# Feed-forward's beginning in a fused attention and FP4 feed-forward kernel: weight pieces turned in order of use, ten before the first gate unit and 24 among the first tile's gate matmuls

## The reference, cut to what matters

```python
x = x + attention(layernorm(x))            # 16 heads, causal, then @ W_O
x = x + ffn(layernorm(x))
def fp4_linear(x, w):                      # x (b, s, k), w (n, k)
    return einsum('bsk,nk->bsn', fp4_quant_dequant(x), fp4_quant_dequant(w))
gate = fp4_linear(x, w_gate)               # w_gate, w_up: 1408 x 512
y = fp4_linear(x, w_up)
h = silu(gate) * y
ffn = fp4_linear(h, w_down)                # w_down: 512 x 1408
```

## Time and profile before

| | us |
|---|---|
| median of 3 runs (lowest, highest) | 3051.26 (3050.97, 3052.30) |
| profiled execution: own time | 3052.97 |
| profiled execution: span in the trace | 3051.2 |
| PE busy in the span | 2989.1 (98%) |
| DVE busy | 2622.9 (86%) |
| ACT busy | 1350.4 (44%) |
| POOL busy | 755.0 (25%) |
| feed-forward's first PE instruction | 1275.29 after the start |

### The profile page before, as it was taken

One profiled execution on the slowest core, in us unless ns is written; L12 is line 12 of the kernel. 1 busy time (PEld: TensorE's weight loads), 2 busy tenths in 40 slices (PEclk: granted clock), 3 DMA queues, 4 the chain that ended last, 5 costly groups with the idle time before them and its releaser, 6 DMA issues.

```text
span 3051.2 us, 65181 instructions
## 1 busy us (share of the span) xinstructions
PE 2989.1 (98%) x23204; PEld 2208.6 (72%) x23204; DVE 2622.9 (86%) x4209; ACT 1350.4 (44%) x2010; POOL 755.0 (25%) x680
## 2 busy tenths in 40 slices
PE   7999899999999999889999999999999999999999
PEld 6787644444444444478888888888888888888887
DVE  7999788889889888888888888888888888888886
ACT  5666577877777787532222222222222222222221
POOL 3444200000000000023333333333333333333332
PEclk9999899999999999999999999999999999999999
DMA  7889856655655665521111111111111111101110
GB/s 244 283 289 300 275 123 143 149 133 137 154 133 138 149 137 137 151 84 32 38 42 42 42 35 35 42 41 42 42 33 36 42 42 41 42 30 40 42 35 15
DMA packets 247628, 304.20 MB, mean 100 GB/s; under 512 B 21968, under 2 KB 154960, under 8 KB 247504
## 3 DMA queue, kind: packets, MB, share of 16 engines
q1 hardware_dynamic: 247504, 302.88, 35.8%
HBM read 190.35 MB, written 112.46 MB: 99 GB/s over the span
## 4 chain that ended last, share of the span: by engine, by line
PE 56%; DVE 1%; ACT 0%; DMA 0%; issue 0%; POOL 0%; SPq 0%; DVEq 0%
PE p_ring L1845 20%; PE p_ring L1873 16%; PE ps_od L1845 11%; PE ps_od L1825 5%; PE p_ring L1863 3%; PE p_ring L1853 1%; DVE sb_wg_lo L1751 0%; PE ps_od L1873 0%; PE p_ring L1825 0%; PE p_ring L1888 0%; DVE sb_fp_tmp L102 0%; DVE sb_wd_lo L1751 0%; DMA dn<-sb_fp_tmp 0%; DVE sb_h_amax L88 0%; DVE sb_stage L1722 0%
## 5 line engine op out<-in xcount | busy, mean ns | idle before, releaser
L1040 ACT ACTIVATE sb_probs<-scores 128x1024 f32<-128x1024 f32 (+3 forms) x512 | 405.8, 840 | 113.7 <-PE scores L1246 107.3
L788 POOL TENSOR_TENSOR sb_at_in<-sb_at_in,sb_inv_in 128x512 f32<-128x512 f32 x64 | 89.0, 1390 | 1069.0 <-DMA sb_inv_in<-dinv 1068.3
L1845 PE MATMUL p_ring<-sb_wg_hi,sb_xq_hi 128*128 128x512 f32 (+1 forms) x1024 | 295.2, 369 | 0.3 <-DVE sb_wd_lo L1751 0.3
L1548 POOL TENSOR_TENSOR sb_stage<-sb_stage,sb_h_inv 128x512 f32<-128x512 f32 (+1 forms) x192 | 210.8, 1098 | 339.2 <-DVE sb_h_inv L94 339.2
L1845 PE MATMUL p_ring<-sb_wg_lo,sb_xq_hi 128*128 128x512 f32 (+1 forms) x1024 | 290.5, 365 | 0.0
L1845 PE MATMUL p_ring<-sb_wg_hi,sb_xq_lo 128*128 128x512 f32 (+1 forms) x1024 | 289.9, 364 | 0.0
L1873 PE MATMUL p_ring<-sb_wd_hi,sb_ht_hi 128*128 128x512 f32 x693 | 275.9, 398 | 0.0
L1246 PEld LDWEIGHTS scores<-sb_q_hi,sb_k_hi 32*128 32x128 f32 x1536 | 73.7, 182 | 278.3 <-ACT sb_probs L1040 154.6
L1873 PE MATMUL p_ring<-sb_wd_hi,sb_ht_lo 128*128 128x512 f32 x693 | 270.2, 390 | 0.0
L1873 PE MATMUL p_ring<-sb_wd_lo,sb_ht_hi 128*128 128x512 f32 x693 | 269.8, 389 | 0.0
L1554 POOL TENSOR_TENSOR sb_stage<-sb_stage,sb_h_scale 128x512 f32<-128x512 f32 (+1 forms) x192 | 190.0, 989 | 267.4 <-DVE sb_stage L104 267.4
(11 more groups left out here) (203 smaller groups left out, 7172.3 us busy)
## 6 DMA issues: line engine op xcount, KB each, us to landing
kq<-sb_kq_out SPq DMA_DIRECT2D x32, 1024.0 KB, 7.2
sb_kq_raw<-kq SPq DMA_DIRECT2D x64, 512.0 KB, 6.8
sb_xin<-in_L_attn_x_dram SPq DMA_DIRECT2D x32, 512.0 KB, 6.9
v<-sb_v_out SPq DMA_DIRECT2D x64, 256.0 KB, 6.5
rq<-sb_r_out SPq DMA_DIRECT2D x64, 256.0 KB, 4.4
sb_qr<-rq SPq DMA_DIRECT2D x32, 512.0 KB
sb_kr_hi<-kr SPq DMA_DIRECT2D x32, 512.0 KB
sb_kr_lo<-kr SPq DMA_DIRECT2D x32, 512.0 KB
```

Of the source, the lines that this page charges most:

```text
L1040: act.activation(probs(k)[:, 2 * pair:2 * pair + 2, off:BANK], scores[(2 * k + pair) % RING2][:, :, off:BANK], ACT.Exp, scale=SCALE).then_ ...
L1548: pool.tensor_tensor(x, x, spread(h_inv[:, a // QB:b // QB], (b - a) // QB), ALU.mult).then_inc(h_y, 1)
L1845: i = pe.matmul(ps[:, m, 0:b0 - a0], xt[a][:, c, :], wg[b][:, m, c, a0:b0], start=(c == 0 and a == b == 0), stop=(c == DC - 1 and a == 1))
```

## The change

The pieces are reordered, so that gate and up pieces for hidden columns 0 to 511 come first (pieces 0 to 7), then those for 512 to 1023 (8 to 15), then the rest (16 to 21); the down pieces stay last. Ten pieces (`ALONE`) are turned in the phase of their own, which now ends with `turn_x(0, 0)`. The other 24 are turned inside tile 0's gate units (`AMONG`): six in G0 (one every two passes), ten in G1 and eight in G2 (one before each of the first passes). Each gate unit waits for the pieces that it needs (`NEEDED`: 8, 16; G2 waits for 26). The wait for all 34 moves to G1 of tile 1. Pieces from 16 on use only the four late slots. G2's pieces use two other banks, and piece 27 waits for the bank of G0.

ACT and DVE get the pieces in matching places of their lists: on ACT, eight pieces stand between `magic_h(0, 0, 0)` and `round_attention(0, 2)`; on DVE, 26 and 27 stand behind `hidden(0, 0, 1)`, and 28 to 33 behind `round_hidden(0, 0, 0)`. For tile 0 POOL runs `hidden_y` of unit 0 before `divide`. SP stores the last rows of attention (which share tiles with `x_to_y`) behind the load of piece 9 instead of 11.

```diff
-FIRST_LATE = 28
-LATE = {28: 7, 29: 8, 30: 9, 31: 10, 32: 2, 33: 1}
+FIRST_LATE = 16
+ALONE = 10
+AMONG = [(ALONE, 16), (16, 26), (26, 34)]
+NEEDED = [8, 16, 22]
...
-    return LATE[n] if n >= FIRST_LATE else n % PREP_SLOTS
+    return PREP_SLOTS + n % LATE_SLOTS if n >= FIRST_LATE else n % PREP_SLOTS
...
-        self.jobs = [(m, r, 0, D) for m in range(2) for r in range(FC)]
+        self.jobs = [(m, r, 0, D) for rows in (range(4), range(4, 8), range(8, FC)) for m in range(2) for r in rows]
...
-            return ring[n % RING3 if n < GATE_JOBS else 1 + n % 2][:, 1]
+            return ring[n % RING3 if n < ALONE else 1 + n % 2 if n < AMONG[2][0] else 2 + n % 2][:, 1]
...
-                if n == 11:
+                if n == 9:
                     sp.wait_ge(o_copied, 1)
                     sp.dma_start(t["at"][B * GROUPS - 1, :, BANK:S], last_o[:]).then_inc(last_stored, 16)
...
+                if flags(q, r)[0]:
+                    hidden_y(q, r, 0)
                 if exists(q, r + 2):
                     divide(q, r + 2)
-                hidden_y(q, r, 0)
+                if not flags(q, r)[0]:
+                    hidden_y(q, r, 0)
...
-            for n in range(GATE_JOBS):
+            for n in range(ALONE):
                 round_job(n)
...
-                if n == 8:
+                if n == 6:
                     magic_x(0, 0)
-                if n == 15:
-                    round_x(0, 0, (0, -1))
+            round_x(0, 0, (0, -1))
...
                 if first:
-                    for n in range(GATE_JOBS, 25):
+                    for n in range(ALONE, 14):
                         round_job(n)
                 if exists(q, r + 1):
                     magic_x(q, r + 1)
                 if first:
-                    for n in range(25, FIRST_LATE):
+                    for n in range(14, AMONG[1][0]):
                         round_job(n)
                 silu_of(q, r, 0)
...
                 if first:
-                    for n in range(FIRST_LATE, len(jobs)):
+                    for n in range(*AMONG[1]):
                         round_job(n)
                 silu_of(q, r, 1)
                 magic_h(q, r, 0)
+                if first:
+                    for n in range(*AMONG[2]):
+                        round_job(n)
                 if exists(q, r + 2):
                     round_attention(q, r + 2)
                 silu_of(q, r, 2)
...
-                if n == 9:
+                if n == 7:
                     x_to_q(0, 0)
-                if n == 17:
-                    rest_of_x(0, 0, (0, -1))
+            rest_of_x(0, 0, (0, -1))
...
                 if first:
-                    for n in range(GATE_JOBS, 24):
+                    for n in range(ALONE, 13):
                         rest_of_job(n)
                 if following:
                     x_to_y(q, r + 1)
                 if first:
-                    for n in range(24, FIRST_LATE):
+                    for n in range(13, AMONG[1][0]):
                         rest_of_job(n)
                 hidden(q, r, 0)
                 if first:
-                    for n in range(FIRST_LATE, 30):
+                    for n in range(AMONG[1][0], 19):
                         rest_of_job(n)
                 if following:
                     x_to_q(q, r + 1)
...
                 if first:
-                    for n in range(30, len(jobs)):
+                    for n in range(19, AMONG[2][0]):
                         rest_of_job(n)
                 hidden(q, r, 1)
+                if first:
+                    for n in range(AMONG[2][0], 28):
+                        rest_of_job(n)
                 round_hidden(q, r, 0)
+                if first:
+                    for n in range(28, len(jobs)):
+                        rest_of_job(n)
                 hidden(q, r, 2)
...
-                if flags(q, r)[0] and s == 2:
+                if flags(q, r)[0]:
+
+                    pe.wait_ge(lo, AMONG[2][0] if s == 2 else NEEDED[s])
+                if isinstance(q, int) and (q, r, s) == (0, 1, 1):
...
-                        if flags(q, r)[0] and s < 2 and at % 2 == 0:
-                            turn_weights(GATE_JOBS + 6 * s + at // 2)
+                        if flags(q, r)[0] and s == 0 and at % 2 == 0:
+                            turn_weights(AMONG[0][0] + at // 2)
+                        if flags(q, r)[0] and s > 0 and at < AMONG[s][1] - AMONG[s][0]:
+                            turn_weights(AMONG[s][0] + at)
...
-                if n >= GATE_JOBS:
-                    pe.wait_ge(lo, max(GATE_JOBS, n - 1))
+                if n == AMONG[2][0] + 1:
+
+                    pe.wait_ge(ps_free, number(0, 0, "G0") + RING3 + 1)
+                elif n >= ALONE:
+                    pe.wait_ge(lo, max(ALONE, n - 1) if n != AMONG[2][0] else n)
...
-            for n in range(GATE_JOBS):
+            for n in range(ALONE):
                 turn_weights(n)
                 if n == 3:
                     project(0, 0, (0, -1))
-                if n == 13:
-                    turn_x(0, 0, (0, -1))
-            pe.wait_ge(lo, GATE_JOBS)
+            turn_x(0, 0, (0, -1))
```

## The result

| | before | after |
|---|---|---|
| median, six runs each on one chip (lowest, highest) | 3051.16 (3049.13, 3053.57) | 3061.97 (3057.34, 3064.26) |
| ratio, 95% interval | | 1.0033 (1.0021 to 1.0046) |
| profiled execution: own time | 3052.97 | 3057.34 |
| profiled execution: span | 3051.2 | 3055.5 |

The account below looks back on a forecast made before the run. DVE was taken to bound the stretch the change touches, PE everything from 1337.5 on. Leads of 6.7, 6.2 and 1.2 us became 5.8 and 9.0 late, then +6.8: span 3058.0, median 3058.1; sum's range 3055.5 to 3060.5, wider 3052.5 to 3062.

Parts of the forecast that it names:

- Signs of being wrong: `hidden` of unit 1 before 1322, a clock of 0.50 inside G1, or `divide` ending before G2 does.
- Phase alone: Stretch up to `residual(0, 1)`: it starts at 1299.0 instead of 1305.71, a lead of 6.7 us.
- G0: Tile 0's first gate unit: ends 1.5 us later; `hidden(0, 0, 0)` at 1310.35 instead of 1316.56, lead 6.2.
- G1: Second gate unit, ten pieces: waits of pieces spend 5 of 6.2 us; lead 1.2 at `hidden(0, 0, 1)`.
- G2: Third gate unit, now eight pieces: ends at 1336.3 against 1330.5, 5.8 us late.
- Tile 2's inputs: Loads queued behind piece 33's: `divide` starts at 1337.8, HT0 of tile 1 at 1346.55, 9.0 us late.
- Given back: HT0 and G0 of tile 1 at full clock take 6.55 instead of 8.81 us, leaving +6.8 us.
- The store: In the phase alone: stored behind piece 9's load, it frees `x_to_y` sooner, 1.0 us saved.
- from there on all as before: Behind HT0 of tile 1, nothing changes up to the kernel's end.
- rival (a): Clock also falls in gaps inside G1 and G2: 2.4 us more, 3060.5; chance 0.24 including late loads.
- rival (c): Faster: the 18 pieces behind G0 hide under matmuls, the 6.2 us lead stays, 3045.0; chance 0.06.
- (b): Piece loops close better and `divide` comes sooner, tile 2's inputs some 3 us earlier: 3054.3; chance 0.25.

Follow-up runs that it names:

- again: The changed kernel run once more without an edit: 3062.52 us, ratio 1.0039 to the kernel before.
- three_banks: The changed kernel with pieces among the gate units rotating over three PSUM half banks instead of two: 3054.74 us, ratio 1.0008 to the kernel before.
- tile2_early: The changed kernel with SP's requests for tile 2 moved ahead of the load of piece 20: 3055.41 us, ratio 1.0010 to the kernel before.
- store_at_9: The kernel before with only the store of attention's last rows moved behind the load of piece 9 instead of 11: 3051.77 us, ratio 1.0000.
- after_last_filled: The changed kernel with seven matmuls, results unread, ahead of the last tile's last `down`: 3058.30 us, ratio 1.0021 to the kernel before.
- before_filled: The kernel before with matmuls, results unread, in PE's gaps up to HT0 of tile 1: 3050.10 us, ratio 0.9994.
- both_last_filled: The changed kernel with tile 2's loads early, three half banks, unread matmuls in early gaps and seven in the last tile: 3048.22 us, ratio 0.9984.
- before_last_filled: The kernel before with unread matmuls in PE's early gaps and seven in the last tile: 3049.80 us, ratio 0.9989.

## Why the prediction was right, and where it fell short

**Direction and chain of steps: right; size: too small.** The kernel became slower, 1.0033, by the steps given, at 10.8 us between the medians instead of 6.8. The interval of that comparison (6.4 to 14.0 us) still holds 6.8; that of "again" (1.0025 to 1.0054) begins at 7.6.

**Signs of being wrong.** Two of the three came true by the letter. `hidden(0, 0, 1)` started at 1321.12, before 1322; but 1322 is 46.7 us after the T0 of before, and it came at 47.11, in an execution whose first 7 us ran at full clock (49.9 with that taken out). That one is the start's luck. The other, 0.50 inside G1, is real, and is treated below.

**Phase alone** (lead 6.7 at `residual(0, 1)`): measured 6.9 with the start's clock taken out (30.42 - 23.5), 6.4 in "again". Two errors cancel within it, which is luck: XT started 0.5 us later than forecast (18.4 after T0 with the 2.8 added, against 18.0), because `x_to_y`'s first instruction ran beside POOL, and the clock came back 3.5 us after XT's start instead of 4.7.

**G0** (lead 6.2): 6.5 and 5.9. **G1** (15.05 us long, so 5 of the 6.2 lost): 15.13 wherever the clock didn't add to it, with gaps of 2.11 and, in "again", 2.02 us released by DVE, as the working has them. The two-bank loop of 2.13 us for two pieces took 2.12 and 2.13 (turns at 1314.19, 1316.31 and 1318.44). three_banks shows the cause: one more bank takes 2.6 us off (2.0 where tile 2's `divide` falls into G1). **G2** (10.9): 10.7, with the turn of 28 2.98 us behind `hidden(0, 0, 1)` (forecast 2.95) and that of 30 5.83 (5.75). DVE released every such wait; the loads into four slots released none.

**Tile 2's inputs**: `divide` 1.5 us after G2's end forecast, 1.95 measured, and all that was queued behind it came in the order given. tile2_early shows its price: 3.5 to 3.9 us. **Given back**: 6.38 us for HT0 and G0 (forecast 6.55), `project(0, 2)` at half clock. HT1 of tile 1: +6.8 forecast, +6.85 in the profile after with the start's clock taken out.

**The store**: 1.0 us saved was forecast. `x_to_y` waited for no transfer and started 7.79 us after T0, 10.6 on before's footing, against 11.70: 1.1 earlier. Its first instruction took 1.05 us instead of 0.55, so 0.6 is left. Started earlier, it runs beside POOL's L1540 (1.27 us from 1281.29), which in the kernel before was done by then; in "again", tile2_early and store_at_9 it takes 1.05 to 1.06 as well. In the kernel before the same edit is worth nothing at the end (store_at_9).

**The term that was mis-sized is TensorE's clock.** The last sentence of the sum, "the span becomes 3051.2 + 6.8", rests on "from there on all as before". It isn't: 1.5 us are lost in the last tile in seven of eleven traces, and before's trace happened to be one of the four without. The second part is rival (a), which the sum put at nothing. Its mechanism exists: the clock fell behind a gap of 2 us in G1 in all four traces with two banks and no filling there (after, again, tile2_early, after_last_filled). Its price was 2.4 us forecast and is 0 in three of them and 1.3 in "again", because a wait of PE for DVE can absorb it.

With 1.3 and 1.56 added, 6.8 becomes 9.7; "again" shows 9.9 from T0 to the end (8.34 + 1.56). That accounts for one trace. For the medians it isn't shown: how many of the other executions paid in G1 isn't known, and the dip of the last tile counts in the difference only as far as the kernel before has it less often. before_filled has it, before and store_at_9 don't. So the 4.0 us between the forecast and the measured medians stay in part open.

**A slip in the prices.** "A turn about 0.36" doesn't follow from the two rows beside it: 0.91 - 0.47 is 0.44. With it the 17.1 us of rival (c) would be 17.7. Nothing else in the sum hangs on it.

**Rivals.** (b), loops that close better, is refuted for this kernel (G1 15.13) and became true in G1 only with a third bank (12.56 and 13.1). (c), faster, needed `hidden(0, 0, 1)` 45.1 us after T0; it came at 47.11 in the execution that started at full clock, 49.9 on before's footing, and 51.79. Even with both faults mended and the gaps filled, G1 takes 13.1 us instead of 10.0: DVE has ten subtractions, `hidden` and `x_to_q` there, as (c)'s own bound says.

**What stays open**: why the clock at T0 differs from run to run (half speed behind waits of 3.4 to 3.5 us, full behind 2.09, 3.25 and 3.33, in between behind 2.20 and 2.27), why the last tile's dip appears in some executions only, and what the rest of the medians' difference is. The first two were seen and priced, not explained. That both_last_filled is better than before_last_filled (3048.22 and 3049.80) isn't shown.
